# Cross attention: probabilities and split context turned by DMA transposes, key split taken from PSUM, scores in four PSUM banks

## The reference

```python
qx = _ln(_fp8_linear_pertensor(ln_out, wqx, ...).reshape(b, s, g, hpg, d), qxln_w, qxln_b)
kvx = jnp.einsum('bsi,oi->bso', cond, w_kv_x)          # cond: [16, 1601, 256]
kx, vx = jnp.split(kvx, 2, axis=-1)
kx = _ln(kx.reshape(b, sc, g, d), kxln_w, kxln_b)
scores = jnp.einsum('bsghd,btgd->bghst', qx, kx) * scale
p = jax.nn.softmax(scores, axis=-1)
xout = jnp.einsum('bghst,btgd->bsghd', p, vx)
```

## Time and profile before

| | us |
|---|---|
| median of 3 runs | 2950.43 |
| lowest and highest run | 2949.21, 2951.61 |
| span of the profiled execution (first to last instruction) | 2952.8 |
| busy in it: TensorE | 2367.6 |
| busy in it: VectorE | 2181.1 |
| busy in it: ScalarE | 1546.8 |
| busy in it: GpSimd | 1535.3 |

### The profile page before, as it was taken

How to read it: one execution, slowest core, us unless ns; L and a number is a source line. 1 busy time by engine, 2 the same in 40 slices (tenths; PEclk the granted TensorE clock), 3 DMA queues, 4 the chain that set the end, 5 groups by cost and what they waited for, 6 DMA issues and landing times. The chain is left out here.

```text
span 2952.8 us, 56699 instructions
## 1 busy us (share of the span) xinstructions
PE 2367.6 (80%) x18770; PEld 1873.2 (63%) x18770; DVE 2181.1 (74%) x4595; ACT 1546.8 (52%) x3121; POOL 1535.3 (52%) x1605
## 2 busy tenths in 40 slices
PE   2456652899999999999999999999999996657665
PEld 0234341777777777777777777777777774535442
DVE  8898884577778677777778777787777774756665
ACT  4555541666666666656656666666666663111111
POOL 2456566667666676666757667676676541000000
PEclk9677776999999999999999999999999998778876
DMA  2010113010101101011010110101100002310100
GB/s 100 15 43 21 43 43 135 17 42 24 42 32 41 32 31 42 25 48 32 24 43 32 40 33 31 42 25 38 42 24 31 9 1 76 141 36 1 36 4 4
DMA packets 55279, 112.03 MB, mean 38 GB/s; under 512 B 4080, under 2 KB 38336, under 8 KB 53824
## 3 DMA queue, kind: packets, MB, share of 16 engines
q1 hardware_dynamic: 54976, 108.25, 10.6%
HBM read 90.42 MB, written 17.83 MB: 37 GB/s over the span
## 5 line engine op out<-in xcount | busy, mean ns | idle before, releaser
L71 PE MATMUL x_kc<-x_wk,x_ctxT 128*128 128x256 f16 x4992 | 627.3, 275 | 70.9 <-POOL x_ctxT L975 40.6
L997 POOL TENSOR_TENSOR x_kT<-x_kf,x_kT 128x512 f16<-128x512 f32 (+1 forms) x448 | 629.9, 1406 | 37.3
L71 PE MATMUL x_ox<-x_ctxp,x_pt 128*128 128x256 f16 x4992 | 620.6, 273 | 0.0
L995 POOL TENSOR_SCALAR x_kT<-x_kf 128x512 f16<-128x512 f32 (+1 forms) x448 | 287.3, 641 | 621.0 <-ACT x_kf L1067 619.2
L71 PEld LDWEIGHTS x_kc<-x_wk,x_ctxT 128*128 128x128 f16 x4992 | 484.6, 99 | 155.6 <-issue 59.3
L71 PEld LDWEIGHTS x_ox<-x_ctxp,x_pt 128*128 128x128 f16 x4992 | 486.5, 98 | 72.9 <-issue 11.4
L1055 ACT ACTIVATE x_kraw<-x_kc 128x512 f32<-128x512 f32 (+1 forms) x448 | 254.2, 567 | 429.4 <-PE x_kc L71 217.0
L1263 DVE TENSOR_REDUCE x_ss<-x_sq 128x4 f32<-128x512 f32 (+1 forms) x448 | 283.1, 643 | 231.9 <-ACT x_sq L1059 230.4
L1320 DVE TENSOR_TENSOR x_pt<-x_tp,x_pt 128x512 f16<-128x512 f32 (+1 forms) x512 | 298.2, 586 | 118.8 <-ACT x_pt L1094 115.4
L1067 ACT ACTIVATE x_kf<-x_tp,x_hv 128x512 f32<-128x512 f32 (+1 forms) x448 | 330.5, 755 | 86.3 <-PE x_tp L1146 85.5
L1181 PE MATMUL x_tp<-x_ident,x_pb 128*128 128x128 f32 x1664 | 257.0, 274 | 56.6 <-ACT x_pb L1088 54.4
(11 more groups left out here) (219 smaller groups left out, 3340.2 us busy)
## 6 DMA issues: line engine op xcount, KB each, us to landing
x_stage<-in_ctxT SPq DMA_DIRECT2D x32, 800.5 KB, 4.4
x_stage<-in_ctx SPq DMA_DIRECT2D x16, 896.0 KB, 5.0
x_stage<-in_ctx SPq DMA_DIRECT2D x16, 640.0 KB
scr_q<-a_qxT SPq DMA_DIRECT2D x8, 1024.0 KB, 3.9
x_qs<-scr_q SPq DMA_DIRECT2D x16, 512.0 KB, 5.3
scr_core<-a_catc SPq DMA_DIRECT2D x8, 512.0 KB, 2.6
scr_x<-x_catx SPq DMA_DIRECT2D x8, 512.0 KB, 2.7
f_cat<-scr_core SPq DMA_DIRECT2D x8, 512.0 KB, 5.6
```

The costliest lines, as they stand in the source:

```text
L71: last = pe.matmul(out, lhs[i], rhs[j], start=start and n == 0, stop=stop and n == len(parts) - 1)
L995: gp.tensor_scalar(dst[0], src, 1.0, 0.0, ALU.mult, ALU.add).then_inc(khi_ready, 1)
L997: gp.tensor_tensor(dst[1], src, dst[0], ALU.subtract).then_inc(kT_ready, 1)
```

## The change

- **Probabilities.** `exp` covers all 1601 columns in one instruction. ScalarE then writes the high f16 part `ph[.., 0]` of the probabilities (`phi`, a new instruction per group), GpSimd the low part `ph[.., 1]` (`low_probs`), both 1601 wide, still with the queries on the partitions. SP turns each part with one DMA transpose of 13 blocks of 128 x 128 into `pt` (`turn_probs`). `pt` on TensorE, ScalarE and VectorE is gone.
- **Context.** It is loaded only as rows; GpSimd splits it into `ctxp` one batch earlier than before, and SP makes `ctxT` from `ctxp` with DMA transposes (`turn_rows`, two per half, four per batch).
- **Keys.** ScalarE writes `kT` high straight from the `tp` bank (`high_k`), VectorE the low part from the same bank (`low_k`); `kf` and GpSimd's split are gone. The key bias is no longer added to the keys: its product with each group's queries is made on TensorE once per batch (`qb`) and added to the maximum.
- **Scores** go to four banks `s4`; `tp` has two banks in place of three. A bank of `tp` with keys is free when VectorE has written the low part.
- **Orders.** `raw` and `sq` are separate entries, the square reads `kraw` from SBUF and not `kc`, and TensorE waits for the copy alone. All `pv` pieces of group 0 stand at the end of the step.

```diff
-        ORDER = [("m", 0), ("sr", 0), ("sc", 0), ("pv", -1, 0), ("pv", -1, 1), ("tr", 0), ("oa", -2), ("m", 1),
...
+        ORDER = [("qb",), ("sc", 0), ("m", 0), ("oa", -2), ("pv", -1, 0), ("tr", 0), ("ob", -2), ("m", 1),
...
+            def turn_rows(b, slot, half):
+                sp.wait_ge(ctx_ready, b * 8 + 4 * half + 4)
...
+                for p in range(2):
+                    sp.dma_start_transpose(ctxT[:, slot, p, lo * KC:hi * KC, :],
+                                           ctxp[:, slot, p, lo:hi, :].rearrange("p c n -> p (c n)")
+                                           ).then_inc(ctxT_ready[half], 16)
...
+            def turn_probs(J, A_):
+                for p, made in enumerate((phi_ready, plo_ready)):
+                    sp.wait_ge(made, J * 2 + A_ + 1)
+                    sp.sem_inc(passed_sp, 1)
+                    if p == 0 and not (isinstance(J, int) and J == 0):
+                        sp.wait_ge(pv_done, J * 2 + A_ - 1)
+                        sp.sem_inc(passed_sp, 1)
+                    sp.dma_start_transpose(pt[:, A_, p], ph[:, A_, p]).then_inc(pt_ready[A_], 16)
...
+                    turn_probs(J, 0)
                     if jj < 2 and not (last(t) and j >= SPB):
...
+                        if not (first(t) and j < SPB):
+                            sp.wait_ge(kc_filled, b * SPB * KU)
+                            sp.sem_inc(passed_sp, 1)
+                        turn_rows(b + 1, (j // SPB + 1) % 2, jj)
+                        if not last(t):
+                            load_rows(b + 2, jj)
...
+                    turn_probs(J, 1)
...
+            def low_probs(J, A_):
+                gp.wait_ge(phi_ready, J * 2 + A_ + 1)
+                if not (isinstance(J, int) and J == 0):
+                    gp.wait_ge(pt_ready[A_], J * 32)
+                gp.sem_inc(passed, 1)
+                gp.tensor_tensor(ph[:, A_, 1, 0:L], pb[:, A_], ph[:, A_, 0, 0:L], ALU.subtract).then_inc(plo_ready, 1)
...
+                    low_probs(J, 0)
+                    if convert_here:
+                        if jj == 0 and not (first(t) and j < SPB):
+                            gp.wait_ge(pv_done, b * 8)
+                        for n in range(2):
+                            convert_piece(jj, slot, b + 1, n)
+                    low_probs(J, 1)
+                    if convert_here:
+                        for n in range(2, 4):
+                            convert_piece(jj, slot, b + 1, n)
...
+                act.activation(kT[:, jk % 2, 0, :, cs[0] * P:cs[0] * P + n],
+                               tp[:, bank, 0:2 * n].rearrange("p (g n) -> p g n", g=2), ACT.Copy, scale=hv[:, 3:4]
+                               ).then_inc(khi_ready, 1)
...
+                    act.activation(pb[:, A_], s4[:, 0:L], ACT.Exp, bias=negm[:, A_:A_ + 1], scale=SOFTMAX_SCALE,
+                                   accum_out=ls[:, j % 2, A_:A_ + 1]).then_inc(probs_ready, 1)
+                elif kind == "phi":
...
+                    act.activation(ph[:, A_, 0, 0:L], pb[:, A_], ACT.Copy).then_inc(phi_ready, 1)
...
+                pe.wait_ge(kraw_ready, 4 + u)
...
+            def low_k(JK, jk, i, bank):
...
+                v.scalar_tensor_tensor(lo, tp[:, bank, 0:2 * n].rearrange("p (g n) -> p g n", g=2), hv[:, 3:4], hi,
+                                       ALU.mult, ALU.subtract).then_inc(kT_ready, 1)
...
+                        pe.wait_ge(pt_ready[A_], 16 * (group - A_) + 32)
```

More of the change, by code:

```diff
@@ L713, in cross_attend @@
         stage = sb("stage", [P, 2, 7 * C])
-        ctxT = sb("ctxT", [P, 2, 2, KC, LP], F16)
+        ctxT = sb("ctxT", [P, 2, 2, CH * KC, P], F16)
         ctxp = sb("ctxp", [P, 2, 2, CH, C], F16)
@@ L729, in cross_attend @@
         yb = sb("yb", [P, NH * S], BF16)
-        eb = sb("eb", [P, NH * S], U16)
+        eb = [y[:, slot].bitcast(U16)[:, 0:NH * S] for slot in range(2)]
         yf = sb("yf", [P, NH * S])
@@ L857, in wait_tp @@
                 if exists(pt_, pj, po):
-                    s, value = read(pt_, pj, po)
+                    s, value = freed(pt_, pj, po)
                     pe.wait_ge(s, value)
@@ L999, in _, with convert_piece @@
-            for i in range(KU):
-                split_unit(0, 0, i)
+            gp.wait_ge(pads_ready, 8)
+            def convert_piece(half, slot, b, n):
+                src, (hi, lo) = list(pieces(half, slot))[n]
+                if n == 0:
+                    gp.wait_ge(stage_ready[half], (32 if half else 16) * (b + 1))
+                gp.sem_inc(passed, 1)
+                gp.tensor_scalar(hi, src, 1.0, 0.0, ALU.mult, ALU.add).then_inc(ctx_hi, 1)
+                gp.wait_ge(ctx_hi, b * 8 + half * 4 + n + 1)
+                gp.tensor_tensor(lo, src, hi, ALU.subtract).then_inc(ctx_ready, 1)
@@ L1002, in tile @@
+            for half in range(2):
+                for n in range(4):
+                    convert_piece(half, 0, 0, n)
+            def low_probs(J, A_):
[4 more added lines that the diff above has]
+                gp.tensor_tensor(ph[:, A_, 1, 0:L], pb[:, A_], ph[:, A_, 0, 0:L], ALU.subtract).then_inc(plo_ready, 1)
             def tile(t):
@@ L1003, in tile @@
                 for j in range(SPT):
[L1004 removed]
+                    J = t * SPT + j
                     jj, b = j % SPB, t * BT + j // SPB
[L1006 to L1024 removed]
@@ new lines, in tile @@
+                    slot = (j // SPB + 1) % 2
+                    convert_here = jj < 2 and not (last(t) and j >= SPB)
+                    low_probs(J, 0)
[8 more added lines that the diff above has]
+                            convert_piece(jj, slot, b + 1, n)
@@ L1135, in project_k @@
                         ins = products(pe, kc[:, n * 256:(n + 1) * 256],
-                                       [ctxT[:, slot, p, k, c * P:(c + 1) * P] for p in range(2)],
+                                       [ctxT[:, slot, p, c * KC + k, :] for p in range(2)],
                                        [wk[:, p, k, gp_ * 256:(gp_ + 1) * 256] for p in range(2)], k == 0, k == KC - 1)
@@ L1193, in part @@
                         c = 4 * i + n
-                        ins = products(pe, ox[:, 0:C], [pt[:, A_, p, c * P:(c + 1) * P] for p in range(2)],
+                        ins = products(pe, ox[:, 0:C], [pt[:, A_, p, c, :] for p in range(2)],
                                        [ctxp[:, slot, p, c, :] for p in range(2)], c == 0, c == CH - 1)
```

321 lines of the change are left out of this document (136 added, 185 removed), and 18 rows, old and new, of tables (ACT_ORDER, DVE_ORDER, ORDER).

## The result

The changed kernel takes **3155.65 us** (median of 4 runs, 3154.53 to 3157.15) where the kernel before took 2951.02 (4 runs, 2949.21 to 2951.82): ratio 1.0697, 95% interval [1.0682, 1.0712]. It is 7% slower. The forecast was 2876 us, a gain; the result is a loss. It lies inside the range of 2830 to 3230, between 3070 and 3230 us, a stretch that the prediction gave a chance of 0.10 as the slow end of its rival on SP's queue.

A forecast was written before the change was run, and what follows sets the result against it. TensorE, busy 94%, was taken as the bound. From the 2952.8 us span, 63 steps going from 30.6 to 29.6 us save 63 and the start 12: 2878, less 2 for the median of runs, 2876 us; range 2830 to 3230.

The forecast's parts named there:

- rival on SP's queue: Above 2.3 us a transpose, group 1's probabilities wait behind context transposes: 2965 to 3070 us, chance 0.22; to 3230, chance 0.10.
- TensorE's content: TensorE's work per cross_attend step falls from 28.0 to 25.4 us: probability transposes leave, bias products come.
- the undisturbed step: An ordinary cross_attend step, without the quantiser or its neighbours' bias products, takes 28.0 us.
- the walk: ScalarE, VectorE and TensorE orders laid side by side through one step: mean 29.2 us, before any late transpose.
- The two new waits: TensorE waits in each step for ScalarE's copy of projection unit 3, 1.4 us, and a tp bank's clearing, 1.3 us.
- The start: Before the first scores: rows come first in the queue, 7 us, and units wait for the copy alone, 5 us; 12 together.
- The step with the quantiser: The cross_attend step with the quantiser's 6 us on VectorE takes 30.8 us.
- The price of a transpose: One DMA transpose of 416 KB takes 1.6 us, plus 1.3 us fixed.
- the chain behind GpSimd's last piece: In a batch's first two steps, four transposes follow that piece: ready at 32.9 against 31.9 wanted, then 31.6, in time.
- 800 KB loads leave the queue: both were hidden: Context term: these loads and GpSimd's ctxT splits go, without effect on the time.
- the break-even formula: Late steps cost 8X - 12.1 us per four steps for X us a transpose, meeting the gain at 2.3; chance 0.06.
- X: Length of one DMA transpose in us; forecast 1.3 to 2.0, with slower cases up to 4.5 and 4.9.

The follow-up runs named there:

- e2_probs_first: The changed kernel with all four probability transposes of a step ahead of context transposes and loads in SP's queue: 2895.21 us, ratio 0.9815 to the kernel before.

## Why the prediction was wrong, step by step

**TensorE's content and the undisturbed step: right.** The undisturbed steps run at 28.4 and 27.8 us, and the walk had 28.0; in the 28 us from 1447 on TensorE is busy 25.80, against 25.4 forecast. The durations hold within a tenth. By form (busy us, mean ns, idle before and its releaser):

```profile
L985 POOL TENSOR_TENSOR x_ph<-x_pb,x_ph 128x1601 f16<-128x1601 f32 x128 | 415.1, 3243 | 1542.4 <-ACT x_ph L1084 1542.4
L1291 DVE SCALAR_TENSOR_TENSOR x_kT<-x_tp,x_hv,x_kT 128x512 f16<-128x512 f32 x384 | 286.6, 746 | 347.6 <-ACT x_kT L1053 347.5
...
L1053 ACT ACTIVATE x_kT<-x_tp,x_hv 128x512 f16<-128x512 f32 x384 | 262.8, 684 | 267.6 <-PE x_tp L1136 267.4
L1311 DVE TENSOR_REDUCE x_m<-x_s 128x1 f32<-128x1601 f32 x128 | 232.8, 1819 | 44.4 <-PE x_s L71 44.4
...
L1077 ACT ACTIVATE x_pb<-x_s,x_negm 128x1601 f32<-128x1601 f32 x128 | 204.5, 1598 | 127.7 <-DVE x_negm L1316 126.2
L1084 ACT ACTIVATE x_ph<-x_pb 128x1601 f16<-128x1601 f32 x128 | 197.2, 1541 | 0.1
```

Forecast were 3.6, 0.69, 0.7, 1.83, 1.61 and 1.6 us. The two new waits were to be 1.4 us on `x_kraw` and 1.3 on `x_kT` a step; the list has 124.9 us in 73 waits (1.7 each, those of 4.3 us in the steps with the quantiser among them) and 56.8 in 51 (1.1 each). In an ordinary step of `e2_probs_first` they are 1.1 and 1.1.

**The start: right**, 12.2 us for 12.

**The step with the quantiser: 1.5 us too short.** 30.8 forecast, 32.3 measured where no transpose is late. The cause is the pass L1346, 2.88 us long beside L985 and 0.68 away from it; moved, it left steps of 30.5 and 30.0. The walk had nothing for one engine's pass stretching another's here.

**The price of a transpose: the hold right where nothing is ahead, the landing too low.** SP's issues of `x_pt` in the changed kernel (ns min/median/max) and their landing:

```profile
L908 SPq DMA_TRANSPOSE x_pt<-x_ph x256: 1285/1486/5742, 533.1 to 2671.3; - x128
...
DMA to landing us min/median/max: 3.8/3.8/8.5
```

The hold of 1.5 us stands against a forecast of 1.6. But one alone lands after 3.8 us, and the sum had 1.3 + 1.6 = 2.9. The fixed 1.3 us, taken from plain copies, should have been 2.3. The hold is no constant: behind the loads it was 3.42 and 2.98 us (above). The figure of the Trainium skill, "DMA: Bandwidth & Descriptors", section "Latency and other measured facts", is 261 GB/s; it lies between the two rates measured here, 213 GB/s for a transpose that moves alone (1388.5 to 1390.0 us) and 289 for two that were queued together (1418 to 1420). The 1309 ns for one 128 x 128 block by DMA that the Trainium skill, "VectorE: DVE Perf Modes", section "The three transpose paths", lists are not what each of 13 blocks costs: together they hold SP for 1.5 us and land after 3.8.

**The step that failed is the chain behind GpSimd's last piece**, "25.0 + 1.3 + 4.15 x 1.6 = 32.9". It counted transposes only. "800 KB loads leave the queue: both were hidden" looked at the loads that go and not at those that stay, which now stand between two things in a hurry. For the second step of a batch, from the last piece's end to what TensorE wants, the sum allowed 31.9 - 24.1 = 7.8 us; measured 1406.07 to 1413.57, 7.5. The chain in that time, forecast and measured:

| | forecast | measured |
|---|---|---|
| two context transposes | 1.85 x 1.6 = 3.0 | 3.6 (1406.07 to 1409.64) |
| plain loads, `x_stage` twice and `x_qs` | 0 | 2.5 (1409.64 to 1412.14) |
| high and low part, until the product can start | 3.2 + 1.3 = 4.5 | 8.6 (1412.14 to 1420.73) |
| sum | 7.5 | 14.7 |

The 7.2 us of difference are the wait of 7.17. Of the 4.1 us in the third row, 1 is the landing from above. The rest is in the longer hold of the first issue (3.5 us to the second issue, not 1.6) and a still later landing of the second (5.0 us), and both go with the DMA traffic of 1412 to 1422 us (GB/s in 40 slices of 0.25 us):

```profile
GB/s 201 266 360 389 377 381 389 287 221 164 246 238 254 272 332 287 208 187 140 96 46 22 198 292 290 290 276 292 290 290 289 293 77 0 0 0 0 0 0 0
```

Of the two transposes' 852 thousand bytes 719 thousand are the last block, 1417.5 to 1420.2, at 290 GB/s. The traffic of the 5 us ahead of it, some 1.2 MB, is nearly all that of the loads. The transposes, issued from 1412.14 on, move from 1415.0: until 1417.3 only 133 thousand bytes of theirs (the packets of 256 bytes) go beside the loads, and the rest when those have ended. A transpose with nothing ahead, issued at 1387.11, moves from 1388.2. So the loads cost their place twice, as issue and as traffic ahead. In the run with the loads behind, the same way took 6.1 us (1491.55 to 1497.63). To this come 2 to 3 us of lower clock a late step, which the sum did not have either.

**The rivals.** The mechanism of "the SP queue behind the context transposes" is the one that came, at its place and in its steps. Its condition was wrong: it was to begin at 2.3 us a transpose, and it began at 1.5, since the break-even formula left out the loads too. The chances were dealt out over a quantity, X, that did not decide; the run with plain copies, which hold SP for 0.47 us, is still 4.4% slower than the kernel before. The measured time fell in the stretch that stood for X of 3.3 to 4.5 us, while X was 1.5: that it lies in the stated range is luck. GpSimd's lateness was in the sum as a given (25.0), never as something with a price: taken out alone it was worth 198 us.

**What stays open.** That the late clock follows from TensorE's wait is read from one stretch and from the change with the wait's length (twelve products 2.74 us long after 7.17, 1.48 after 2.44), not tested apart. The walk's mean agrees with the 29.65 us of `e2_probs_first`, but partly by chance: there no transpose is late, and the quantiser's step is 1.5 us longer.

## What to carry to other kernels

Write down every instruction of an in-order queue between the moment a result is ready and the moment its successor is issued, the plain loads and the waits too, before asking how long the new operation takes. When a DMA takes over work that was in an engine's own order, put it ahead of all that is not urgent on its queue, and let what that queue waits for be made early by the engine that has idle time: here the first turned a 7% loss into a gain of 1.9%, the second into a loss of 0.4%. The first check of such a kernel is the list of periods: undisturbed steps at the forecast length send the search to what the other steps have besides.
